# Unread products of the mask and the identity on TensorE between the last attention chunk and the first expert

## The reference, cut to what matters

```python
x = x + tanh(g_xattn) * xattn(layernorm(x), ctx)      # 16 heads of 32, causal, then Wout
x = x + tanh(g_ffn)   * ffn(layernorm(x))
def ffn(h):
    route = sigmoid(h @ router_w)                     # 8 experts
    e, p  = argmax(route), max(route)                 # each token goes to one expert
    return p * ((silu(h @ gate_w[e]) * (h @ up_w[e])) @ down_w[e])
```

## Time and profile before

| what | before |
|---|---|
| runs, us | 570.88, 570.38, 569.41 (median 570.38) |
| profiled execution, us | 570.18 |
| its span, us | 568.7 |
| TensorE busy in the span | 519.9 us (91%) |
| VectorE, ScalarE, GpSimd busy | 355.4, 308.1, 184.4 us |
| mean granted TensorE clock | 0.966 |

### The profile page before, as it was taken

The page is one execution under the profiler, slowest core; times in us unless marked ns, Lnnn a source line. Parts: engine busy times, 40 slices in busy tenths (PEclk is TensorE's granted clock), DMA queues, the critical chain, the costliest instruction groups (busy, mean ns, idle before and its releaser), DMA issues.

```text
span 568.7 us, 11407 instructions
## 1 busy us (share of the span) xinstructions
PE 519.9 (91%) x3724; PEld 439.8 (77%) x3724; DVE 355.4 (63%) x745; ACT 308.1 (54%) x855; POOL 184.4 (32%) x210
## 2 busy tenths in 40 slices
PE   1999999999899999955799999999999999999991
PEld 1966786768576856645689999999999999999981
DVE  3677658756875475777165765666666665766731
ACT  1799658765786487322154555454454554554530
POOL 5534305533563245351421422224122321330211
PEclk9999999999999999985699999999999999999997
DMA  7500032103310031182456666668657587575610
GB/s 200 164 1 2 16 88 87 61 17 86 87 58 14 15 89 59 35 276 64 99 172 221 217 198 219 218 201 269 204 195 227 168 280 243 170 240 178 213 59 29
DMA packets 58910, 77.31 MB, mean 136 GB/s; under 512 B 5398, under 2 KB 40830, under 8 KB 58880
## 3 DMA queue, kind: packets, MB, share of 16 engines
q1 hardware_dynamic: 53728, 66.90, 38.2%
q0 software_dynamic: 5152, 10.03, 5.4%
HBM read 68.81 MB, written 10.86 MB: 140 GB/s over the span
## 4 chain that ended last, share of the span: by engine, by line
PE 72%; DVE 7%; issue 6%; ACT 5%; POOL 3%; DMA 2%; DVEq 0%; ACTq 0%; SPq 0%; POOLq 0%
PE bank L1147 20%; PE bank L1149 20%; PE bank L1148 20%; ACT pr L667 3%; POOL pn L507 3%; PE bank L1242 2%; PE bank L1232 2%; DMA staging<-in_L_xattn_Wq 2%; PE bank L1281 1%; PE bank L1401 1%; PE bank L1168 1%; PE bank L1251 1%; ACT staging L611 1%; PE bank L1289 1%; DVE pT L969 1%
## 5 line engine op out<-in xcount | busy, mean ns | idle before, releaser
L1147 PE MATMUL bank<-x_hi,gu_hi 128*128 128x256 f32 x512 | 145.2, 284 | 2.5 <-DVE x_lo L780 1.4
L1148 PE MATMUL bank<-x_lo,gu_hi 128*128 128x256 f32 x512 | 144.8, 283 | 0.0
L1149 PE MATMUL bank<-x_hi,gu_lo 128*128 128x256 f32 x512 | 144.8, 283 | 0.0
L1147 PEld LDWEIGHTS bank<-x_hi,gu_hi 128*128 128x128 f32 x512 | 97.8, 191 | 4.0 <-DVE x_lo L780 1.8
L1148 PEld LDWEIGHTS bank<-x_lo,gu_hi 128*128 128x128 f32 x512 | 97.4, 190 | 0.8
L1149 PEld LDWEIGHTS bank<-x_hi,gu_lo 128*128 128x128 f32 x512 | 97.8, 191 | 0.0
L667 ACT ACTIVATE pr<-bank,nmx 100x100 f32<-100x100 f32 x256 | 85.5, 372 | 15.6 <-DVE nmx L960 12.1
L780 DVE TENSOR_TENSOR gu_lo<-staging,gu_hi 128x1024 fp32r<-128x1024 f32 x64 | 76.5, 1220 | 7.6 <-ACT gu_hi L611 6.4
L507 POOL TENSOR_TENSOR pn<-pr,inv 100x400 f32<-100x400 f32 x64 | 54.7, 854 | 77.8 <-DVE inv L953 72.6
L611 ACT ACTIVATE gu_hi<-staging 128x1024 fp32r<-128x1024 f32 x64 | 65.7, 1051 | 18.4 <-DMA staging<-in_L_ffn_up_w 12.2
L667 ACT ACTIVATION_READ_ACCUMULATOR pr<-bank,nmx 100x1 f32 x256 | 59.8, 235 | 0.0
(11 more groups left out here) (182 smaller groups left out, 978.9 us busy)
## 6 DMA issues: line engine op xcount, KB each, us to landing
staging<-in_L_ffn_gate_w SPq DMA_DIRECT2D x32, 512.0 KB
staging<-in_L_ffn_up_w SPq DMA_DIRECT2D x32, 512.0 KB, 6.6
staging<-in_L_ffn_down_w SPq DMA_DIRECT2D x32, 512.0 KB
x_rows<-x SPq DMA_DIRECT2D x8, 800.0 KB
xt<-in_x SPq DMA_DIRECT2D x4, 800.0 KB
xr<-in_x SPq DMA_DIRECT2D x16, 200.0 KB
staging<-in_L_xattn_Wq SPq DMA_DIRECT2D x1, 1024.0 KB, 10.5
x<-in_L_xattn_Wout SPq DMA_DIRECT2D x1, 1024.0 KB, 9.3
```

The source lines that it names most:

```text
L1147: nc.tensor.matmul(dst, a[0], b[0], start=first, stop=False)
L1148: nc.tensor.matmul(dst, a[0], b[1], start=False, stop=False)
L1149: return nc.tensor.matmul(dst, a[1], b[0], start=False, stop=last)
```

## The change

A helper `keep_clock(bank, count)` issues `count` products of the identity and the mask into a bank, without a wait and without a semaphore. Nobody reads them. The banks used are overwritten later by TensorE itself, or are not in use then. The helper is called at seven places; 10 + 13 + 5 + 16 + 9 + 38 + 8 = 99 products are added. Nothing is removed and no wait is changed.

```diff
             attend(NCH - 1, False, True)
+            def keep_clock(bank, count):
+                for _ in range(count):
+                    nc.tensor.matmul(bank[0:S, 0:HP * S], eye[0:S, 0:S], mask[0:S].unsqueeze(1).to_broadcast([S, HP, S]),
+                                     start=True, stop=True)
+
+            idle_b = turn_b[0], out_b[1]
             pe.wait_ge(rank_used.sem, rank_used.after(NCH - 1, 0))
+            keep_clock(idle_b[0], 10)
             for part in last_parts:
                 if part.number:
+                    keep_clock(idle_b[0], 13)
                     rank(NCH - 1, last_parts[0])
+                    keep_clock(idle_b[0], 5)
                 for i in range(part.first, part.stop):
                     turn_normed(NCH - 1, i, True, last_row_b[i])
                 route_part(NCH - 1, part)
             find(last_parts[0])
+            keep_clock(idle_b[1], 16)
             rank(NCH - 1, last_parts[1])
+            keep_clock(idle_b[1], 9)
             find(last_parts[1])
+            keep_clock(idle_b[1], 38)
...
             turn_tokens(0)
+            keep_clock(gate_b[0], 8)
             gate_up(0, 0)
             pe.wait_ge(units_loaded, 16)
```

## The result

| | before | with the products |
|---|---|---|
| median of 22 runs each, side by side, us | 570.49 | 572.41 |
| lowest and highest, us | 567.72, 572.21 | 569.68, 577.90 |
| ratio of the times, 95% interval | | 1.0049 [1.0029, 1.0070] |
| profiled execution (span), us | 570.18 (568.7) | 571.85 (570.2) |

The account below looks back on a forecast made before the run. TensorE bounds the end from 290 on; its loop entry is held by GpSimd's load of the units. From 570.18, -1.0 for earlier units and +2.0 for half clock behind the gap give 571.2 us; 8-in-10 range 567.8 to 575.6.

Parts of the forecast that it names:

- The prediction's own sign of being wrong: Clock at 0.50 anywhere between 250 and 275, a short idle stretch before the loop, or the loop starting before the units land.
- -1.0 and +2.0: Earlier load of the table of units, -1.0 us; half clock behind the gap before the loop, +2.0 us (bounds 0 and 2.9).
- slower by over 0.3%: Whole kernel above 572.1 us: the stage's fall plus the upper fifth of the forecast, chance 0.30.
- no difference: Whole kernel within 0.3% (1.7 us) of before, between 568.7 and 572.1 us, chance 0.53.
- Part 0, 1.1 us sooner: Routing stage, part 0: router block shrinks from 2.59 to about 1.5 us, so VectorE's choice comes 1.1 sooner.
- Part 1, 2.0 sooner: Routing stage, part 1: faster transposes and router block add at most 0.9 us; choice 1 comes 2.0 sooner.
- The 13 and the 5 hidden: Routing stage: 13 products fit a 2.40 us gap; 5 take 0.9 us against 0.95 available, just hidden.
- The 16 late by 1.1: Ahead of part 1's `rank`: 16 unread products make it wait 1.1 us after `hot`; bounds 0 and 1.9.
- The units 1.0 us sooner: GpSimd's path: `idx_next`, gather, four scatters and load of the units come 1.0 us sooner; bounds 0.3 and 2.1.
- The loop is held by the units, not by ScalarE: Loop entry at 285.51: TensorE waits for `units_loaded`; the rival that TensorE's path decides gave 566.0 us, chance 0.08.
- A gap of 4.3, the clock falls, 2.0 us: Before the loop: TensorE stands 4.3 us, clock falls in or just behind the gap, costing 2.0 us.
- The rival of the stage's fall: Padded routing stage: clock falls inside it, 16 products take 5.8 us, units 3.4 later; 575.6 us, chance 0.22.

## Why the prediction was right or wrong

The time (572.41 against 571.2) lies in the range, and the direction was right; the size was low by 1.2 us. Of the mechanism one half held: the loop is held by the units, TensorE idles before it, the clock falls and the loss goes to the end. The other half didn't. The prediction's own sign of being wrong, a clock of 0.50 anywhere between 250 and 275, was met (251.3 to 254.7), and the units, which were to come 1.0 us sooner, came 0.73 later, counted as in the table. Of its two terms, -1.0 and +2.0, the profile shows +0.70 and +1.49: misses of 1.7 and 0.5 in opposite directions, so that the total is nearer than the parts is in some measure luck. The interval of the ratio reaches from 0.29% to 0.7%, so slower by over 0.3%, to which I gave 0.30, was the better call than no difference, which had 0.53.

- *Part 0, 1.1 us sooner*: 1.03. *Part 1, 2.0 sooner*: 1.67. The router block at full clock, priced 1.5 from the transposes' ratio, is 1.58 and 1.62.
- *The 13 and the 5 hidden*: wrong. The clock fell at 251.3 among the 13, they took 4.06 in place of 2.3, and the transposes of part 1 came not at all sooner. I had put this fall into a rival as a matter of whole executions, and gave the forecast a clock of 1.00 up to 280.
- *The 16 late by 1.1*: right in kind, 1.66 in size (`hot` done at 260.34, `rank` at 262.00). Halving the block gave 1.35 us back.
- *The units 1.0 us sooner*: this is the term that failed. The gather came 0.29 sooner and the load of the units 0.73 later: 0.71 of the miss lies ahead of the gather, with the 13, the 5 and the 16, and 1.02 behind it. I carried GpSimd's path from gather to load as a constant; the scatter of the table took 6.3 us to land, not 5.3. The same issue took 3.2 to 8.1 us in other orders. Why it rose here is open: in GpSimd's old order it took 5.3, 5.5 and 5.9 without products in the routing stage and 6.3, 6.9, 6.6 and 4.6 with them. One rival stands untested: from 278 to 280 weights of the first expert move at nearly 370 GB/s in both traces, and the scatter, issued 0.90 sooner after, lands behind them at the same moment (282.3 and 282.4).

```profile
278.00:280.00 2.00, 2.00 (x11) 0.50 1.06 368
```
```profile
278.00:280.00 2.00, 2.00 (x19) 1.00 1.07 369
```
- *The loop is held by the units, not by ScalarE*: right. In seven traces with the old order the loop's first matmul stands 2.9 to 3.3 us behind the load's issue, and with the load ahead of the scatters the wait is gone.
- *A gap of 4.3, the clock falls, 2.0 us*: 5.08, it fell at 285.5, and the quarter lost 1.49. That a gap of 1.12 left it alone was no safe row to build on: it fell with gaps of 1.99 and 1.53 in two kernels above and held with 1.26 and 1.59 in two others.
- *The rival of the stage's fall, 573 to 578, chance 0.22*: it is a second way in which single executions go, seen in one trace of another kernel (8 for 16 and the units first: 3.6 us late at the gather, forecast 3.4) and in the mean clock of the slowest executions of the change (577.6 us at 0.968, 577.9 at 0.976 of the 22), of which there is no trace. Ten of the 22 lie in its range of 573 to 578; by their mean clocks it may be five of them (0.979 or less, where the profiled one has 0.987). It belonged in the sum with its share and not beside it.

The Trainium skill, "TensorE: Matmul & The Clock Gate", says in its section on the PE-mode transpose that transposes don't engage the full clock, as they don't count as busy in the same way. The experiment with six more products agrees in part: the fall came after a stretch of transposes and router blocks in which TensorE was never idle. The start of the kernel before speaks against it as a rule: 24 transposes after 12.7 us of idleness run (5.35-0.42)/23 = 0.21 us apart, the 16 at 18.43, with only transposes before them, (1.54-0.25)/15 = 0.09 apart, and the first form again at 20.68 0.11 apart. The levels are read from these steps alone, as the granted clock stands at 1.00 in the profile from 0 on, through the 12.7 us of idleness too.

```profile
12.71 5.35 PE L1168 MATMUL bank<-ident,staging 128*128 128x128 f32 x24 [12.71 <-DMA staging<-in_L_xattn_Wq]
...
18.43 1.54 PE L1185 MATMUL bank<-ident,xn 100*128 100x100 f32 x16
...
20.68 1.91 PE L1168 MATMUL bank<-ident,x 128*128 128x128 f32 x16
```

The 24 have 128 rows by 128 columns; the routing stage has transposes of 100 by 100 and router blocks of 8 columns. Which of these differences matters, if any, was not tried.

## What to carry to other kernels

Work that keeps a clock up has to stand where nobody waits for what follows it: its length doubles in exactly the executions in which it fails, and here 16 products in a gap with room for about half of them took back 1.59 of the 1.67 us that the faster blocks had given. Before speeding an engine up towards a point, find what else arrives there at the same moment; here the units' load, and half an expert later the second unit's rows, took whatever TensorE won. Before reading a difference of half a microsecond from one trace of each kernel, look how much the traces of kernels that don't differ there differ. The name that a profile gives to a wait can be wrong when two paths arrive together: read the code's wait, and look for the issue and landing of the DMA behind it.

## What was not expected of the hardware

- A DMA of 0.1 KB took 1.7 to 2.1 us when it was issued after the scatter ahead of it had landed, and 5.3 and 5.9 behind four scatters and a store issued just before it from the same engine. Issuing it 3.1 and 4.2 us sooner gained nothing.
- The clock fell behind a gap of 1.53 us (286.8) and one of 1.99 (285.3) and held over one of 1.59.
- TensorE lost its full clock at 251.3 though it had been busy without a pause of over 0.2 us from 246.35 on, with transposes and router blocks for the last 2.6 us before the 13 products.
- A product of 400 columns takes 0.17 to 0.18 us to the next at full clock and about 0.34 at half, whatever is done with it: unread work has the full price of its columns.
